# A causal-attention layer on eight cores: a planner's constant for slipping fill matmuls between attention units goes from 4.0 to 3.8

## What is computed

```
xn = layernorm(x)
q, k, v = (xn @ wq.T + bq) / 8, xn @ wk.T + bk, xn @ wv.T + bv      # 16 heads of 64
s = softmax(q @ k.T + causal mask) @ v;  s = s @ wo.T + bo
g = silu(xn @ weight.T + pooled(xn) @ disha)
out = x + s * g
```

## Time and profile before

| | us |
|---|---|
| the two timed runs | 780.22 and 834.47 |
| their median | 807.34 |
| the profiled execution, its own time | 781.82 |
| the profiled execution, span of its slowest core (core 6) | 780.3 |
| spans of the eight cores in it | 769.8 to 780.3 |

### The profile page before, as it was taken

How to read it: one execution, slowest core, us unless ns; L and a number is a source line. 1 busy time by engine, 2 the same in 40 slices (tenths; PEclk the granted TensorE clock), 3 DMA queues, 4 the chain that set the end, 5 groups by cost and what they waited for, 6 DMA issues and landing times.

```text
span 780.3 us, 8777 instructions; the slowest of 8 cores (769.8 to 780.3 us)
## 1 busy us (share of the span) xinstructions
PE 644.8 (83%) x2784; PEld 238.1 (31%) x2784; DVE 251.6 (32%) x372; ACT 336.3 (43%) x387; POOL 102.7 (13%) x164
## 2 busy tenths in 40 slices
PE   0444999999999999776688888989999988994975
PEld 0433444444333444221122222222222222221321
DVE  5856644444333100022412232222231111124454
ACT  0322000000000233656366679887778898881000
POOL 0000000000000000343022322221212111111111
PEclk9999999999999999755588899997789999997878
DMA  6322510110100000300020001001200100014212
GB/s 196 92 74 64 148 54 1 54 55 5 51 1 0 1 0 1 115 22 21 7 68 15 28 28 35 17 32 41 61 8 8 35 20 27 22 35 110 86 54 95
DMA packets 25696, 34.86 MB, mean 45 GB/s; under 512 B 4898, under 2 KB 19362, under 8 KB 25652
## 3 DMA queue, kind: packets, MB, share of 16 engines
q1 hardware_dynamic: 23092, 25.91, 12.1%
q0 software_dynamic: 2560, 8.39, 2.8%
HBM read 21.63 MB, written 8.39 MB: 38 GB/s over the span
## 4 chain that ended last, share of the span: by engine, by line
PE 67%; DVE 16%; DMA 5%; issue 5%; ACT 4%; SPq 1%; DVEq 1%; POOL 0%; ACTq 0%; POOLq 0%
PE PS L345 13%; PE PS L682 12%; PE PS L643 11%; PE PS L686 8%; PE PS L370 7%; PE PS L394 7%; PE Q L505 5%; ACT PT L656 4%; DVE OddB L577 3%; DVE OddA L575 3%; DMA out<-esb 2%; DVE AttnOT L471 2%; DVE xn L233 2%; DVE st L208 1%; DVE st L210 1%
## 5 line engine op out<-in xcount | busy, mean ns | idle before, releaser
L656 ACT ACTIVATE PT<-PS,neg 128x1024 f16<-128x1024 f32 (+1 forms) x320 | 295.4, 989 | 90.4 <-PE PS L647 88.4
L665 POOL TENSOR_TENSOR PT<-PT,tri 128x256 f16<-128x256 f16 x128 | 85.3, 677 | 610.8 <-ACT PT L656 606.8
L682 PE MATMUL PS<-PT,Vp 128*65 128x512 f16 (+1 forms) x320 | 130.8, 409 | 39.6 <-DVE OddB L577 39.4
L643 PE MATMUL PS<-QT,KT 64*128 64x512 f16 (+1 forms) x320 | 122.4, 383 | 13.4 <-ACT PT L656 11.3
L686 PE MATMUL PS<-PT,Vp 128*65 128x512 f16 (+1 forms) x320 | 124.9, 390 | 0.0
L647 PE MATMUL PS<-QT,KT 64*128 64x512 f16 (+1 forms) x320 | 123.4, 387 | 0.0
L345 PE MATMUL PS<-xnT,wsb 128*128 128x512 f16 x512 | 112.6, 383 | 1.4 <-DVE QT L355 1.4
L575 DVE CAST OddA<-PS 65x512 f16<-65x512 f32 x32 | 22.0, 687 | 256.7 <-PE PS L686 224.3
L400 ACT ACT_TABLE_LOAD x1 | 1.3, 1283 | 183.3 <-PE PS L394 183.3
L505 PE MATMUL Q<-woT,AttnOT 128*128 128x512 f16 x256 | 75.7, 412 | 2.7 <-DVE AttnOT L471 2.2
L643 PEld LDWEIGHTS PS<-QT,KT 64*128 64x128 f16 x320 | 30.0, 94 | 145.2 <-issue 145.0
(11 more groups left out here) (39 smaller groups left out, 347.4 us busy)
## 6 DMA issues: line engine op xcount, KB each, us to landing
out<-esb POOLq DMA_DIRECT2D x32, 256.0 KB, 2.3
xin<-x SPq DMA_DIRECT2D x16, 256.0 KB, 4.0
wbig<-wT SPq DMA_DIRECT2D x8, 512.0 KB, 7.3
QT<-x SPq DMA_DIRECT2D x32, 128.0 KB, 3.0
wsb<-wqT SPq DMA_DIRECT2D x2, 1024.0 KB, 8.9
wsb<-wkT SPq DMA_DIRECT2D x2, 1024.0 KB, 5.3
wsb<-wvT SPq DMA_DIRECT2D x2, 1024.0 KB, 5.2
woT<-woT SPq DMA_DIRECT2D x1, 2048.0 KB, 11.1
```

The costliest lines, as they stand in the source:

```text
L643: g.matmul(PS6[:, 2 * par_ + 0, o:o + n], KT[0:64, p_, sb2:sb2 + NP], QT[0:64, p_, t + o:t + 512], start=True, stop=True),
L656: g.activation(PT[sl_][:, :, o:o + n], PS6[:, 2 * par_:2 * par_ + 2, o:o + n], AF.Exp, bias=neg2[:]), waits=we, inc="sACT")
L665: g.tensor_tensor(PT[sl_][:, :, o:o + NP], PT[sl_][:, :, o:o + NP], t, ALU.mult),
L682: S.emit("tensor", lambda g: g.matmul(psO(0, 65, 0, o, o + n), Vp[:, s_, (2 * p_) * 65:(2 * p_) * 65 + 65], PT[sl_][:, 0, o:o + n], start= ...
```

## The change

One constant in the planner's credit is different. No instruction is added, removed or changed; what can differ is the place at which fill chunks are emitted among the units.

```diff
                     FS["credit"] = min(CCAP, FS["credit"]
-                                       + (172.0 + 2 * N) / 1.2 - 4.0 * N / 2.4)
+                                       + (172.0 + 2 * N) / 1.2 - 3.8 * N / 2.4)
                     while FS["credit"] >= CHUNK:
                         if not pop_chunk():
                             break
```

## The result

The changed kernel takes 776.12 us (median of 11 runs, 772.07 to 778.42), the kernel before 782.84 us (median of 10; the 807.34 quoted ahead was the median of the first two of them). The ratio is 0.9927 with a 95% interval of 0.9905 to 0.9949: by it the change is 5.7 us faster, where 12.5 were forecast. The time lies in the forecast's range and the difference is under the 2% that was to be told from no change but clear of the noise. In some executions one half of the chip shows a lower clock than the other: the medians here count them, the ratios leave them out, and a profile is read on a core of the other half.

What follows compares the result with a forecast made beforehand. In the attention PE (0.88 us a unit) and ACT (0.95) had little left; the drain, PE and DVE alternating, set the end. Drain -16, attention +8.5, clock -5 make -12.5 us: 781.82 to 769.3 us, range 760 to 783.

Steps and rivals of the forecast that it cites:

- How much moves: Fill matmuls by block: 37 leave the drain, 7 to block 1, 15 each to blocks 2 and 3; 121 stay.
- What the drain loses: Drain: leftover fill runs inside PE's 9.80 us wait, three E tiles remain, block 3's first starts earlier; 16 us saved.
- What the attention pays: Attention: 37 moved matmuls at 0.23 us each lengthen it by 8.5 us (0 to 16.6).
- What the clock does: Block 2 and block 3's first pair: one thin pair instead of three, so 5 us of 9.2 back; block 1 put at 0.
- thin pairs: Attention pairs with the least fill, in block 2 those with 6, 4 and 5 matmuls, where the clock fell.
- a clock under 0.9 in block 3 for long: Block 3: one of the signs named as showing the prediction wrong.
- The first: Rival, attention: the clock stays up and some moved matmuls lie in PE's waits; -21.5, 760 us; 24%.
- The third: Rival, block 3: the clock falls in the fifth and sixth pair, moved matmuls cost 0.45 us; +11.6, 793 us; 6%.
- The second: Rival, attention: every chunk delays scores and exponential, 13 us paid and nothing back; 779 us; 17%.
- The fifth: Rival, blocks 2 and 3: denser work on eight cores lowers the clock to 0.78 to 0.89; +26, 808 us; 1%.
- The fourth: Rival, planner: credit is lost at the cap while the queue's head is not ready, so nothing changes; 781.8 us; 2%.

Runs made afterwards that it cites:

- i_before_n_pad: The kernel before (4.0) with the N matmuls padded with zeros to 128 rows: 773.74 us, ratio 0.9894.
- g_n_pad: The changed kernel (3.8) with the N matmuls padded with zeros to 128 rows: 763.42 us, ratio 0.9727 to the kernel before.
- k_e_shallow: g_n_pad with the 8 matmuls of each E tile reading only 16 of their 128 rows: 819.36 us, median of three.
- f_36_n_half: The changed kernel with the constant at 3.6 and N chunks of blocks 1 and 2 at half the credit: 780.26 us, ratio 0.9958.

## Why the prediction was right and wrong

- **How much moves: right.** 44, 66 and 89 matmuls and 121 in the drain were to come, and came.
- **What the drain loses: right.** 16 us were forecast, 16.5 measured on the mean core, with the wait and the E tiles after it as worked out. (Of the four slices read as having ACT at 0 the first has 1; nothing rests on it.)
- **What the attention pays: rather too high.** The step took 0.23 us for a moved matmul, 8.5 in all. With the clock mostly out of the way, i_before_n_pad against g_n_pad, 30 more matmuls made blocks 2 and 3 longer by 3.2 us (243.2 to 246.4), 0.11 each; that is one profile of each, and g_n_pad's is of its fastest run. Full-clock pairs of block 3 from 7 to 13 matmuls give 0.19. At 0.11 to 0.19, 37 are some 4 to 7 us.
- **What the clock does: this step failed.** It said that thin pairs lose the clock, that there would be one in block 2 instead of three, and took 5 us back. The count came true, 5 and 7 matmuls in the fifth and sixth pair and 9 in the others, and the clock did not follow it: pairs with 9 fell in block 2, and with 8 and 11 in block 3. Blocks 2 and 3 took 12.0 us more, of which 30 moved matmuls at 0.11 to 0.19 are 3 to 6: so 6 to 9 us went to the clock, 11 to 14 from what was forecast. The sign that the prediction named for this, a clock under 0.9 in block 3 for long, came in two pairs, 0.76 and 0.83 over 41.85 us. In block 1, put at 0, 2.5 us were gained. The count of fill matmuls in a pair was the wrong thing to look at. In the kernel before, N tiles stood at the end of block 2, and most of block 2's own were left for the drain; now both sets of eight stand inside a block. They are 16 rows deep, and once the clock has fallen among them it comes back late: in the fifth pair of block 3 it stayed down through 10.30 us of a busy PE. With the same counts in the same places, padding them took 29 of the 39.3 us at the lower clock away in the profiled run, and the ratio to the kernel before from 0.9927 to 0.9727.
- **The rivals.** The first, that the clock stays up, had 760 us, and this is near what the padded kernel does, not the changed one. The third had the place: the fifth and sixth pair of block 3 took 21.50 and 20.35 us where 17 is usual, 7.9 together. But it put the price of the other matmuls at 0.45, so its 793 us did not come. The second had a plausible time, 779, for a wrong reason. The fifth did not happen: with padded N matmuls block 3 ran at 0.99 on core 0 with the same fill, and 1.00 and 0.50 are the only levels in the clock records of the profiles here, so no level between them, which it rests on, was seen. The fourth did not happen either: the counts moved as said.

Without the shallow matmuls the change gains what was forecast: 4.0 against 3.8, both padded, is 773.74 against 763.42 us, or 13 us by the two ratios, where 12.5 were forecast. That they agree so closely is in part luck: block 1 gave 3.6 us of it, which the forecast put at 0, and the moved matmuls cost less.

Not settled: what starts a fall. On core 7 of the changed kernel the falls in blocks 2 and 3 begin 5 to 8 us into a pair, about where the last, short units of the pair before are done and PE waits for DVE (1.16 us, just ahead of the fall at 650.33), but in which pair differs between cores that run the same instructions, and with all fill deep some 10 us of it are left in blocks 2 and 3. Why a second N matmul shortened the low time at 3.8 and lengthened it at 4.0 wasn't tried further, nor was why pairs of E tiles alone kept the clock better once the N tiles were padded.

## What to carry to other kernels

When work is moved out of a tail into a stretch that overlaps engines, work out the tail's saving from its timeline, as here, but look at what kind of matmul lands where: a run of shallow ones can hold the clock low with PE fully busy, and a busy share does not show it. A matmul that uses few rows can be padded with zeros at no time of its own (0.38 us at full clock either way); here that was worth more than the change to the changed kernel, and as much to the one before. A planner's constant is best tried again once such a cause is gone: 3.7 with padding won, 3.6 without it (N chunks at half the credit) lost most of what 3.8 had gained that way.

## What the runs showed of the hardware that was not expected

In k_e_shallow 72 matmuls of at most 16 rows ran without a gap for 30.87 us at 0.50 of the clock without getting it back; with 128 rows the clock was back after the first tile. In f_36_n_half PE was busy for 20.50 of 20.50 us at 0.50, with a 16-row matmul in most units. Zeros count: 112 rows of zeros beside 16 rows of data were enough to change the granted clock, so the added rows need hold no data. A 16-row matmul starts 0.31 us after a 128-row one at full clock, a padded one 0.22 us. And the same fill matmuls in the drain took 70.60 us at a clock of 0.55 when 16 rows deep, and 56.30 us at 0.84 when 128 rows deep.
